# Moving the rounding of the quantised tiles in the loop from VectorE to ScalarE

## Chip, cores and metric

One core of one Trainium2 chip runs the kernel. The metric is the device time of the whole program in microseconds (us), lower is better; the time of a kernel is the median of its runs.

## What is computed

Input `x` has 4 batches of 1024 rows of width 512. Two layers follow each other. The first is a gated feed-forward layer with a quantised second half; the second is a small adapter whose weights depend on the batch.

```python
h = x * ((cond @ norm_w.T + 1)[:, None, :] * rsqrt(mean(x * x) + EPS))
val, gate = split(h @ up_w.T, 2)                    # up_w: 4096 x 512
h = val * gelu(gate)                                # 2048 wide
scale = 127 / clip(max(abs(h), axis=-1), 1e-5)      # one scale per row
hq = clip(round(h * scale), -128, 127) / scale      # act_quant
x1 = hq @ weight_quant(down_w).T + x                # 2048 -> 512
Wd_b = Wd + 0.1 * (cond @ Wdd.T + bdd)              # per batch, as for Wu_b
out = x1 + relu(x1 @ Wd_b.T + bd) @ Wu_b.T + bu
```

The step that matters here is `round(h * scale)`. The kernel rounds by adding and then subtracting 1.5 * 2^23 (`ROUND`) in float32. The result is an integer that bf16 holds exactly, so the second product runs in bf16.

## The kernel before, in words

The 4096 rows of `x` are worked on in eight chunks (c = 0 to 7) of 512 rows. Within a chunk, 16 steps (j = 0 to 15) each make one 128 x 512 tile of `h`. Chunk 0 also prepares the weights. Chunks 1 to 6 are three iterations of a loop with two chunks in its body, and chunk 7 stands behind the loop. The quantisation and the down projection of a chunk are done while the next chunk's steps run: tiles of chunk c-1 are quantised in steps 0 to 7 of chunk c, two tiles a step, and multiplied by the down weights in steps 9 to 12.

Each engine has its own queue, and its order is written out by hand (`run` in each engine's block). In a step of chunks 1 to 6 it is as follows.

- **TensorE** (`run`, L953): twelve float16 products for the gate tile (`up_products`, L889 to L895), then twelve for the value tile. It needs the gelu of two steps before (L965) and the `h` tile of two steps before (L987), because the PSUM tiles have two buffers each. In step 0, `turn_absrun` and `spread_scales` stand behind the two halves. In steps 7, 9, 11, 13 and 15 `delta_products` (L897 to L907) follows the value tile; it waits until VectorE has transposed four units of adapter weights (`nat_turned`). In steps 9 to 12 come 16 bf16 products of the down projection (L950), which wait for all of `q_done` (L943).
- **ScalarE** (`run`, L498): gelu of the gate tile into `g` (L507), in step 0 then the copy of the scales (`copy_scales`, L488), then `abs` of the finished `h` tile into the same `g` buffer (L516), which waits for `h_done`. In steps 2 to 5 it also squares a tile of the next `x` (L454), in steps 7 and 8 it scales two of them (L459).
- **VectorE** (`run`, L699): first the transposes of adapter weights (`turn_nat`, L675): in chunks 1 to 6 two instructions in each of steps 4 to 7 and four in each of steps 8 to 15; in chunk 7 only steps 8 to 11 have any. Then `quantise` (L655) in steps 0 to 7: two products by the scale (L660) and two roundings that add and subtract in one instruction and write bf16 (L663). Then the product of value, descale and gelu into `h[j]` (L739), which waits for TensorE, for the gelu and, because it overwrites the tile of the chunk before, for `q_done` of tile j (L738). Then the running maximum of `abs` (L751), which waits for ScalarE's `abs_done`.
- **SyncE** starts the DMAs; it reloads a buffer of adapter weights when it has been transposed (L337).

The tiles of the last chunk are quantised behind the loop by `quantise_last` on VectorE (L830) and `round_tiles` on ScalarE (L570): VectorE rounds the even tiles, ScalarE the odd ones, each in two ACTIVATE instructions.

Of the kernel before, what the change touches and what calls it, by code (L numbers as in the profile page):

```python
# [9 lines left out]
ALU = mybir.AluOpType  # L10
ACT = mybir.ActivationFunctionType
# [4 lines left out]
ROUND = 1.5 * 2.0 ** 23  # L16
# [6 lines left out]
def conditioned_block(nc, x, cond, norm_w, up_w, down_w, Wd, bd, Wu, bu, Wdd, bdd, Wdu, bdu, out):  # L23
# [6 lines left out]
    NCH = N // CH  # L30
    TT = CH // P
    KD = D // P
    FT = FF // P
# [14 lines left out]
    with ExitStack() as ctx:  # L48
        def sb(name, shape, dt):
            return ctx.enter_context(nc.sbuf_tensor(name, shape, dt))  # L50

        def sem(name):
            return ctx.enter_context(nc.semaphore(name))
# [10 lines left out]
        h = sb("h", [P, FT, CH], F32)  # L64
        qreg = sb("qreg", [P, FT * CH // 2], F32)
        q = qreg[:, :].bitcast(BF16).rearrange("p (f t) -> p f t", f=FT)
# [54 lines left out]
        def piece(p):  # L121
            o = 3072 + (p % 2) * 512
            return qreg[:, o:o + 512]
# [4 lines left out]
        def down_rows(dt):  # L128
            o = (4, 8, 12, 8)[dt]
            return h[:, o:o + 4, :].rearrange("p a b -> p (a b)")  # L130
# [44 lines left out]
        h_scaled, q_done = sem("h_scaled"), sem("q_done")  # L175
# [10 lines left out]
        round_added, q_done_act = sem("round_added"), sem("q_done_act")  # L186
# [11 lines left out]
        def squares_in(c, j):  # L198
            return [t for t, a in enumerate((0, 0, 1, 1) if is_first(c) else (2, 3, 4, 5)) if a == j]

        def scalings_in(c, j):
            return [t for t, a in enumerate((2, 2, 3, 3) if is_first(c) else (7, 7, 8, 8)) if a == j]

        def turn_in(c, j):
            k = j - (4 if is_first(c) else 10)
            return [k] if 0 <= k < KD else []
# [4 lines left out]
        def is_first(c):  # L211
            return isinstance(c, int) and c == 0
# [17 lines left out]
        def batch_at(c, last, j):  # L230
            return [u // 4 for u in units_at(c, last, j) if u % 4 == 3]

        def batch_of(i, par, beta):
            k = beta if par else LOOP_UNITS // 4 + beta
            return 10 * i + k, k % 2, 5 * i + k // 2
# [211 lines left out]
        def _(act):  # L447
            def square_x(n, par, t):
                if is_first(n):
                    act.wait_ge(x0_in[t], 16)  # L450
                elif t == 0:
                    act.wait_ge(x_in, 16 * n)
                    act.wait_ge(x_rstd, n)
                act.activation(xl[:, par, t, :].bitcast(BF16), xn[:, t, :], ACT.Square, accum_out=ss[:, t:t + 1]).then_inc(x_squared, 1)  # L454

            def scale_x(n, t):
                if t == 0:
                    act.wait_ge(x_rstd, n + 1)
                act.activation(xn[:, t, :], xn[:, t, :], ACT.Copy, scale=rstd[:, t:t + 1]).then_inc(x_scaled, 1)  # L459

            def x_hi(c, par, k):
                if k == 0:
                    act.wait_ge(sc_copied, c + 2)
                act.wait_ge(ta_full, ta_x(c, k) + 1)
                act.activation(xh[:, par, k, :], x_bank(c, k)[:, :], ACT.Copy, scale=sc_now[:, k:k + 1]).then_inc(x_hi_done, 1)  # L465

            def w_square(jj):
                act.wait_ge(upn_in[jj % 3], 32 * (jj // 3 + 1))
                for i in range(2):
                    m = 2 * jj + i  # L470
                    if m > 0:
                        act.wait_ge(w_squared, m)
                    act.activation(xr[:, 1, :], upn(jj, i), ACT.Square, accum_out=wss[:, m:m + 1]).then_inc(w_squared, 1)

            def w_hi_half(jj):
                for i in range(2):
                    m, ft = 2 * jj + i, jj + FT * i
                    act.wait_ge(w_turned, m + 1)
                    act.activation(w_hi[:, :, ft * P:(ft + 1) * P],
                                   w_bank(jj)[i][:, :].rearrange("p (k f) -> p k f", k=KD), ACT.Copy).then_inc(w_hi_done, 1)  # L480

            def copy_pieces(i):
                dt, f0 = i // 2, 8 * (i % 2)
                act.wait_ge(ta_full, TA_PIECE + i + 1)
                act.activation(wqT[:, f0:f0 + 8, dt * P:(dt + 1) * P],
                               TA[:, :].bitcast(BF16).rearrange("p (f d) -> p f d", f=8), ACT.Copy).then_inc(ta_freed, 1)

            def copy_scales(c):  # L488
                act.wait_ge(s_turned, c + 1)
                act.activation(s_bc[:, :], TB[:, :], ACT.Copy).then_inc(s_bc_done, 1)  # L490
# [7 lines left out]
            def run(c, par, b, i):  # L498
                first, last = is_first(c), b is None
                for j in range(FT):  # L500
                    n = FT * c + j
                    act.wait_ge(gate_full, n + 1)
                    if first:
                        act.wait_ge(desc_done, max(1, j - 1))
                    if not (first and j < 2):
                        act.wait_ge(max_done, n - 1)
                    act.activation(g[:, j % 2, :], GATE[j % 2][:, :], ACT.Gelu,  # L507
                                   scale=desc[:, 2 * j + 1:2 * j + 2]).then_inc(gelu_done, 1)
                    if first and j + 2 < FT:
                        w_hi_half(j + 2)  # L510
                    if first and j + 3 < FT:
                        w_square(j + 3)
                    if not first and j == 0:
                        copy_scales(c - 1)
                    act.wait_ge(h_done, n + 1)
                    act.activation(g[:, j % 2, :], h[:, j, :], ACT.Abs).then_inc(abs_done, 1)  # L516
                    if not last:
                        for t in squares_in(c, j):
                            square_x(c + 1, 1 - par, t)
                        for t in scalings_in(c, j):  # L520
                            scale_x(c + 1, t)
                        for k in turn_in(c, j):
                            x_hi(c, 1 - par, k)
                    if first and 7 <= j < 15:
                        for p in (2 * (j - 7), 2 * (j - 7) + 1):
                            act.wait_ge(piece_in[p % 2], 16 * (p // 2 + 1))
                            if p == 0:
                                act.wait_ge(mean_step, 3)
                            act.activation(piece(p), piece(p), ACT.Copy, scale=wtot[:, 2:3], bias=ROUND).then_inc(piece_biased, 1)
                    if first and j >= 8:  # L530
                        copy_pieces(j - 8)
                    if first and j < 6:
                        for m in {4: (4, 5), 5: (6, 7)}.get(j, (j,)):
                            act.wait_ge(rows_in[m // 2], 16)
                            half = down_rows(m // 2)[:, FF // 2 * (m % 2):FF // 2 * (m % 2 + 1)]
                            act.activation(half, half, ACT.Abs, accum_out=wabs[:, m:m + 1]).then_inc(rows_summed, 1)
                    for beta in batch_at(c, last, j):
                        if batch_of(i, par, beta)[1] == 1:
                            read_sums(i, par, beta)
# [30 lines left out]
            def round_tiles(m0, m1):  # L570
                for m in range(m0, m1):
                    k = 2 * m + 1
                    act.wait_ge(h_scaled, FT * (NCH - 1) + k + 1)
                    act.activation(h[:, k, :], h[:, k, :], ACT.Copy, bias=ROUND).then_inc(round_added, 1)
                    act.wait_ge(round_added, m + 1)
                    act.activation(q[:, k, :], h[:, k, :], ACT.Copy, bias=-ROUND).then_inc(q_done_act, 1)

            act.wait_ge(bd_in, 16)
            copy_x1(0, 0)
            copy_x1(1, 1, (0, 1))  # L580
            copy_scales(NCH - 1)
            copy_x1(1, 1, (2, 3))
            round_tiles(0, 1)
# [13 lines left out]
        def _(dve):  # L597
# [57 lines left out]
            def quantise(c, k0):  # L655
                if k0 == 0:
                    dve.wait_ge(s_bc_done, c + 1)

                for k in (k0, k0 + 1):
                    dve.tensor_tensor(h[:, k, :], h[:, k, :], s_bc[:, :], ALU.mult).then_inc(h_scaled, 1)  # L660
                for k in (k0, k0 + 1):
                    dve.wait_ge(h_scaled, FT * c + k + 1)
                    dve.tensor_scalar(q[:, k, :], h[:, k, :], ROUND, ROUND, ALU.add, ALU.subtract).then_inc(q_done, 1)  # L663

            def quant_pieces(i):
                for p in (2 * i, 2 * i + 1):
# [445 lines left out]
```

## Time and profile before

| what | value |
|---|---|
| median of 3 runs | 1034.6 us |
| lowest, highest | 1031.19, 1034.74 us |
| the profiled execution, its own time | 1033.38 us |
| its span in the trace | 1031.6 us |
| mean granted TensorE clock | 0.993 of full speed |
| busy: TensorE, VectorE, ScalarE | 966.2, 681.9, 329.8 us |

The span is the time between the first and the last instruction in the trace; the execution's own time has 1.8 us around it. Busy time of TensorE comes from modelled ends of pipelined instructions, so consecutive matmuls overlap in the records: what a matmul costs is the distance from its start to the next one's. The same holds in a smaller measure on VectorE and ScalarE, where an instruction may start before the end of the one ahead of it. In timelines, equal instructions that follow each other are merged (x2, x4) and the time given is from the first start to the last end.

### The profile page before, as it was taken

What the parts mean: (1) busy time and instruction counts of PE and PEld (TensorE: products, weight loads), DVE (VectorE), ACT (ScalarE), POOL (GpSimd) and SP (SyncE); (2) the same over time, 40 slices, a digit from 0 to 9 for tenths busy, and PEclk for the clock granted to TensorE, in tenths of its full rate; (3) what the DMA queues carried; (4) which work ended last, traced back from release to release, by engine and by line L of the source; (5) the groups of instructions that cost most, each with busy time, mean ns of one, the idle gap of its engine ahead of it and who ended that gap; (6) DMA issues with size and microseconds to landing.
All of it is one profiled execution on the core that took longest, in us unless ns stands there. A gap on an engine that the chain in (4) does not pass through costs nothing.

```text
span 1031.6 us, 14604 instructions
## 1 busy us (share of the span) xinstructions
PE 966.2 (94%) x5307; PEld 467.7 (45%) x5307; DVE 681.9 (66%) x1138; ACT 329.8 (32%) x599; POOL 51.3 (5%) x53
## 2 busy tenths in 40 slices
PE   1899999999999989999999899999999999987998
PEld 1555544444444444444444344444444444444454
DVE  1878758766785748766885658756876677428433
ACT  2797832312321222212322223222332222115222
POOL 1000000000000000000000000000000000004153
PEclk9999999999999999999999999999999999989999
DMA  7442341545145412454145412544154512232365
GB/s 275 142 151 88 121 144 62 183 144 163 42 153 152 153 66 85 161 162 145 42 165 164 150 45 92 173 155 133 51 173 155 166 69 82 72 112 82 142 227 182
DMA packets 73314, 134.70 MB, mean 131 GB/s; under 512 B 5268, under 2 KB 10904, under 8 KB 72728
## 3 DMA queue, kind: packets, MB, share of 16 engines
q1 hardware_dynamic: 73240, 133.72, 39.5%
q8 instruction: 46, 0.75, 0.3%
q14 instruction: 28, 0.23, 0.1%
HBM read 112.72 MB, written 20.97 MB: 130 GB/s over the span
## 4 chain that ended last, share of the span: by engine, by line
PE 74%; DVE 15%; issue 6%; ACT 2%; SPq 2%; DMA 1%; DVEq 0%; POOL 0%; ACTq 0%; POOLq 0%
PE bank L892 16%; PE bank L893 16%; PE bank L894 16%; PE bank L950 10%; DVE natT L681 8%; PE bank L905 6%; PE bank L1063 2%; PE bank L1048 2%; DVE h L739 2%; DVE h L660 2%; PE bank L877 1%; PE bank L867 1%; ACT g L516 1%; PE bank L1039 1%; DVE h L833 1%
## 5 line engine op out<-in xcount | busy, mean ns | idle before, releaser
L892 PE MATMUL bank<-x_split,w_hi 128*128 128x512 f16 x1024 | 390.4, 381 | 10.0 <-issue 7.4
L893 PE MATMUL bank<-x_split,w_hi 128*128 128x512 f16 x1024 | 390.0, 381 | 0.0
L894 PE MATMUL bank<-x_split,w_lo 128*128 128x512 f16 x1024 | 389.8, 381 | 0.0
L681 DVE STREAM_TRANSPOSE natT<-nat 128x512 f32<-128x512 f32 x256 | 249.6, 1087 | 1.2 <-PE bank L905 0.8
L516 ACT ACTIVATE g<-h 128x512 f32<-128x512 f32 x128 | 80.6, 630 | 362.3 <-DVE h L739 362.3
L739 DVE SCALAR_TENSOR_TENSOR h<-bank,desc,g 128x512 f32<-128x512 f32 x128 | 94.8, 740 | 106.0 <-issue 66.3
L892 PEld LDWEIGHTS bank<-x_split,w_hi 128*128 128x128 f16 x1024 | 100.7, 98 | 129.9 <-issue 17.3
L894 PEld LDWEIGHTS bank<-x_split,w_lo 128*128 128x128 f16 x1024 | 100.7, 98 | 122.2 <-issue 2.5
L507 ACT ACTIVATE g<-bank,desc 128x512 f32<-128x512 f32 x128 | 87.3, 682 | 208.6 <-PE bank L894 208.6
L893 PEld LDWEIGHTS bank<-x_split,w_hi 128*128 128x128 f16 x1024 | 100.7, 98 | 115.1 <-issue 1.9
L751 DVE TENSOR_TENSOR absrun<-absrun,g 128x512 f32<-128x512 f32 x120 | 83.0, 691 | 75.1 <-ACT g L516 75.1
L950 PE MATMUL bank<-wqT,qreg 128*128 128x512 bf16 x512 | 115.3, 379 | 0.0
L660 DVE TENSOR_TENSOR h<-h,s_bc 128x512 f32<-128x512 f32 x112 | 71.6, 680 | 15.5 <-ACT s_bc L490 15.5
L905 PE MATMUL bank<-natT,cond_diag 128*32 128x256 f32 x1024 | 61.9, 382 | 18.1 <-DVE natT L681 18.1
L950 PEld LDWEIGHTS bank<-wqT,qreg 128*128 128x128 bf16 x512 | 49.5, 98 | 57.5 <-issue 3.3
L905 PEld LDWEIGHTS bank<-natT,cond_diag 128*32 128x32 f32 x1024 | 30.3, 109 | 49.2 <-issue 18.7
L828 DVE TENSOR_TENSOR w_hi<-bank,w_hi 128x512 f32<-128x512 f32 x32 | 21.7, 687 | 34.0 <-PE bank L1063 34.0
L421 POOL TENSOR_TENSOR rstd<-ss,mhalf 128x4 f32<-128x4 f32 x8 | 8.1, 1014 | 725.3 <-DVE ss L630 713.6
L663 DVE TENSOR_SCALAR qreg<-h 128x512 bf16<-128x512 f32 x112 | 42.0, 417 | 0.0
L1063 PE MATMUL bank<-natT,w_lo 128*128 128x512 f32 x64 | 30.7, 609 | 4.8 <-DVE w_hi L828 4.1
L696 DVE SCALAR_TENSOR_TENSOR xr<-bank,fy,xr 128x512 f32<-128x512 f32 x32 | 22.3, 697 | 17.8 <-PE bank L950 10.9
L641 DVE SCALAR_TENSOR_TENSOR x_split<-bank,sc_now,x_split 128x512 f16<-128x512 f32 x32 | 23.6, 746 | 12.9 <-ACT x_split L465 12.9
(118 smaller groups left out, 543.7 us busy)
## 6 DMA issues: line engine op xcount, KB each, us to landing
nat<-in_L_cond_Wdd SPq DMA_DIRECT2D x64, 512.0 KB, 3.6
nat<-in_L_cond_Wdu SPq DMA_DIRECT2D x64, 512.0 KB, 3.5
qreg<-in_L_cond_up_w SPq DMA_DIRECT2D x32, 256.0 KB, 4.3
xr<-in_x SPq DMA_DIRECT2D x32, 256.0 KB, 4.6
x_scratch<-xr SPq DMA_DIRECT2D x32, 256.0 KB, 4.8
xn<-in_x SPq DMA_DIRECT2D x7, 1024.0 KB, 6.4
out_y<-w_hi SPq DMA_DIRECT2D x7, 1024.0 KB, 4.3
h<-in_L_cond_down_w SPq DMA_DIRECT2D x4, 1024.0 KB, 7.6
```

The costliest lines, as they stand in the source:

```text
L507: act.activation(g[:, j % 2, :], GATE[j % 2][:, :], ACT.Gelu, scale=desc[:, 2 * j + 1:2 * j + 2]).then_inc(gelu_done, 1)
L516: act.activation(g[:, j % 2, :], h[:, j, :], ACT.Abs).then_inc(abs_done, 1)
L660: dve.tensor_tensor(h[:, k, :], h[:, k, :], s_bc[:, :], ALU.mult).then_inc(h_scaled, 1)
L681: last = dve.transpose(natT[:, t, kk, :, :].rearrange("p a (r e) -> p e a r", e=4), nat[:, t, kk, :])
L739: dve.scalar_tensor_tensor(h[:, j, :], VAL[j % 2][:, :], desc[:, 2 * j:2 * j + 1], g[:, j % 2, :], ALU.mult, ALU.mult).then_inc(h_done, 1)
L751: dve.tensor_tensor(absrun[:, :], absrun[:, :], g[:, j % 2, :], ALU.max).then_inc(max_done, 1)
L892: pe.matmul(bank[:, :], w_hi[:, k, cols], xh[:, par, k, :], start=(k == 0), stop=False)
L893: pe.matmul(bank[:, :], w_hi[:, k, cols], xl[:, par, k, :], start=False, stop=False)
L894: mm = pe.matmul(bank[:, :], w_lo[:, k, cols], xh[:, par, k, :], start=False, stop=(k == KD - 1))
L905: mm = pe.matmul(HY[32 * t:32 * t + 32, cols], cond_diag[:, a, :], natT[:, t, :, a, :], start=(a == 0), stop=(a == HB - 1))
L950: mm = pe.matmul(bank[:, :], q[:, f, t * P:(t + 1) * P], wqT[:, f, :], start=(f == 0), stop=(f == FT - 1))
L1063: pe.matmul(up_bank[t][:, :], down_T[:, par, t * P:(t + 1) * P], wu_all[:, b, :], start=True, stop=True).then_inc(up_full, 1)
```

## The change

VectorE's two rounding instructions of each pair of tiles are gone. ScalarE gets, in steps 0 to 7 of chunks 1 to 7, four instructions per step between its gelu (in step 0: behind the copy of the scales) and its `abs`: add `ROUND` in place in float32 for both tiles, then subtract it into the bf16 tile for both. Each addition waits for VectorE's product of that tile, each subtraction for its own addition. `q_done` is now counted up by ScalarE. The tiles of the last chunk are quantised as before; only the count that `round_tiles` waits for starts at another base, since the loop now counts the same semaphore.

```diff
--- before.py
+++ after.py
@@ -485,6 +485,14 @@
                 act.activation(wqT[:, f0:f0 + 8, dt * P:(dt + 1) * P],
                                TA[:, :].bitcast(BF16).rearrange("p (f d) -> p f d", f=8), ACT.Copy).then_inc(ta_freed, 1)
 
+            def round_pair(c, k0):
+                for k in (k0, k0 + 1):
+                    act.wait_ge(h_scaled, FT * c + k + 1)
+                    act.activation(h[:, k, :], h[:, k, :], ACT.Copy, bias=ROUND).then_inc(round_added, 1)
+                for k in (k0, k0 + 1):
+                    act.wait_ge(round_added, FT * c + k + 1)
+                    act.activation(q[:, k, :], h[:, k, :], ACT.Copy, bias=-ROUND).then_inc(q_done, 1)
+
             def copy_scales(c):
                 act.wait_ge(s_turned, c + 1)
                 act.activation(s_bc[:, :], TB[:, :], ACT.Copy).then_inc(s_bc_done, 1)
@@ -512,6 +520,8 @@
                         w_square(j + 3)
                     if not first and j == 0:
                         copy_scales(c - 1)
+                    if not first and j < 8:
+                        round_pair(c - 1, 2 * j)
                     act.wait_ge(h_done, n + 1)
                     act.activation(g[:, j % 2, :], h[:, j, :], ACT.Abs).then_inc(abs_done, 1)
                     if not last:
@@ -572,7 +582,7 @@
                     k = 2 * m + 1
                     act.wait_ge(h_scaled, FT * (NCH - 1) + k + 1)
                     act.activation(h[:, k, :], h[:, k, :], ACT.Copy, bias=ROUND).then_inc(round_added, 1)
-                    act.wait_ge(round_added, m + 1)
+                    act.wait_ge(round_added, FT * (NCH - 1) + m + 1)
                     act.activation(q[:, k, :], h[:, k, :], ACT.Copy, bias=-ROUND).then_inc(q_done_act, 1)
 
             act.wait_ge(bd_in, 16)
@@ -658,9 +668,6 @@
 
                 for k in (k0, k0 + 1):
                     dve.tensor_tensor(h[:, k, :], h[:, k, :], s_bc[:, :], ALU.mult).then_inc(h_scaled, 1)
-                for k in (k0, k0 + 1):
-                    dve.wait_ge(h_scaled, FT * c + k + 1)
-                    dve.tensor_scalar(q[:, k, :], h[:, k, :], ROUND, ROUND, ALU.add, ALU.subtract).then_inc(q_done, 1)
 
             def quant_pieces(i):
                 for p in (2 * i, 2 * i + 1):
```

## Rows read from the trace of the kernel before

**Rows 1.** Page, part 1: engine, busy us (share of span) xinstructions.

```profile
PE 966.2 (94%) x5307; PEld 467.7 (45%) x5307; DVE 681.9 (66%) x1138; ACT 329.8 (32%) x599; POOL 51.3 (5%) x53
```

**Rows 2.** Groups by line: busy us, mean ns of one | idle before, releaser.

```profile
L905 PE MATMUL bank<-natT,cond_diag 128*32 128x256 f32 x1024 | 61.9, 382 | 18.1 <-DVE natT L681 18.1
...
L663 DVE TENSOR_SCALAR qreg<-h 128x512 bf16<-128x512 f32 x112 | 42.0, 417 | 0.0
```

**Rows 3.** TensorE's waits in chunk 3 (365:478 us): total us, times, longest.

```profile
PE bank L905 <- DVE natT L681: 2.8, 3, 1.0
```

**Rows 4.** TensorE's timeline, chunk 3: start us, us, instruction [idle before <-releaser].

```profile
409.60 1.93 PE L905 MATMUL bank<-natT,cond_diag 128*32 128x256 f32 x32 [0.95 <-DVE natT L681]
411.47 0.39 PE L892 MATMUL bank<-x_split,w_hi 128*128 128x512 f16 x1
...
422.93 1.93 PE L905 MATMUL bank<-natT,cond_diag 128*32 128x256 f32 x32 [0.93 <-DVE natT L681]
```

**Rows 5.** VectorE's timeline, chunk 3, steps 4 to 10.

```profile
389.47 0.69 DVE L751 TENSOR_TENSOR absrun<-absrun,g 128x512 f32<-128x512 f32 x1 [0.69 <-ACT g L516]
390.08 2.03 DVE L681 STREAM_TRANSPOSE natT<-nat 128x512 f32<-128x512 f32 x2
391.94 1.27 DVE L660 TENSOR_TENSOR h<-h,s_bc 128x512 f32<-128x512 f32 x2
...
393.79 0.74 DVE L739 SCALAR_TENSOR_TENSOR h<-bank,desc,g 128x512 f32<-128x512 f32 x1
395.23 0.69 DVE L751 TENSOR_TENSOR absrun<-absrun,g 128x512 f32<-128x512 f32 x1 [0.70 <-ACT g L516]
...
412.59 0.69 DVE L751 TENSOR_TENSOR absrun<-absrun,g 128x512 f32<-128x512 f32 x1 [0.70 <-ACT g L516]
...
433.69 0.75 DVE L739 SCALAR_TENSOR_TENSOR h<-bank,desc,g 128x512 f32<-128x512 f32 x1 [4.28 <-PE bank L894]
```

**Rows 6.** ScalarE's timeline, chunk 3, steps 3 and 4.

```profile
388.81 0.63 ACT L516 ACTIVATE g<-h 128x512 f32<-128x512 f32 x1 [2.74 <-DVE h L739]
389.34 0.61 ACT L454 ACTIVATE x_split<-xn 128x512 bf16<-128x512 f32 x1
...
394.57 0.63 ACT L516 ACTIVATE g<-h 128x512 f32<-128x512 f32 x1 [3.32 <-DVE h L739]
```

**Rows 7.** ScalarE's timeline after the loop: its own roundings.

```profile
943.09 0.63 ACT L574 ACTIVATE h<-h 128x512 f32<-128x512 f32 x1 [1.45 <-DVE h L833]
943.75 0.63 ACT L576 ACTIVATE qreg<-h 128x512 bf16<-128x512 f32 x1
```

**Rows 8.** ScalarE's timeline after the last step: four PSUM copies in a row.

```profile
934.24 2.05 ACT L562 ACTIVATE w_hi<-bank 128x512 f32<-128x512 f32 x4
```

**Rows 9.** VectorE's timeline, chunk 3, steps 0 to 3.

```profile
373.06 1.29 DVE L660 TENSOR_TENSOR h<-h,s_bc 128x512 f32<-128x512 f32 x2 [2.21 <-ACT s_bc L490]
...
376.38 0.43 DVE L748 COPY absrun<-g 128x512 f32<-128x512 f32 x1 [0.69 <-ACT g L516]
376.72 1.29 DVE L660 TENSOR_TENSOR h<-h,s_bc 128x512 f32<-128x512 f32 x2
...
382.84 0.75 DVE L739 SCALAR_TENSOR_TENSOR h<-bank,desc,g 128x512 f32<-128x512 f32 x1 [0.24 <-issue]
...
388.02 0.75 DVE L739 SCALAR_TENSOR_TENSOR h<-bank,desc,g 128x512 f32<-128x512 f32 x1 [1.17 <-issue]
```

**Rows 10.** VectorE's timeline, last chunk, step 4.

```profile
847.06 0.75 DVE L739 SCALAR_TENSOR_TENSOR h<-bank,desc,g 128x512 f32<-128x512 f32 x1 [1.17 <-issue]
```

**Rows 11.** TensorE's timeline at the start of chunk 3, after its longest idle time.

```profile
364.49 0.38 PE L892 MATMUL bank<-x_split,w_hi 128*128 128x512 f16 x1 [4.09 <-issue]
...
368.76 0.60 PE L930 MATMUL bank<-identf,absrun 128*128 128x128 f32 x4
```

**Rows 12.** Windows: busy us (x) of each engine, granted clock, DMA share, GB/s.

```profile
365.00:370.00 5.00, 5.00 (x19) 2.18 (x18) 0.60 (x1) 0.69 (x1) 0.00 (x0) 0.66 0.40 152
...
405.00:410.00 5.00, 4.05 (x25) 1.76 (x27) 4.30 (x8) 1.21 (x2) 0.00 (x0) 1.00 0.33 102
```

## The prediction

> **What bounds the kernel now.** The page's part 1 comes first [rows 1]: TensorE is busy 94% of the span, VectorE 66%, ScalarE 32%. So only TensorE's idle time can be won, and only new idle time on it can be lost; work moved from VectorE to ScalarE is worth what it changes there. The groups by line say who makes TensorE wait in the loop [rows 2]: the adapter products L905 lose 18.1 us to VectorE's transposes. One chunk's waits [rows 3] show the pattern: three stops, 2.8 us together. The other loop chunks repeat it.
>
> TensorE's timeline gives the places [rows 4]: 0.95 us idle before the L905 group of step 7, 0.93 us before that of step 9. It also gives its pace: from 411.47 to the idle time's start (422.00) run the 48 products of steps 8 and 9; the last starts 0.38 us before its modelled end, so 47 distances fill 10.15 us, 0.216 us each. A step of 24 takes 5.18 us.
>
> VectorE's timeline says why it is late [rows 5]. The running maximum L751 starts at 389.47 in step 3, at 395.23 in step 4 and at 412.59 in step 7: 5.76 to 5.80 us a step against TensorE's 5.18. These steps are a ring of two engines with no wait for TensorE in it: maximum, 0.61 us later two transposes, 1.86 later the two products by the scale, 1.85 later the h pass L739, then ScalarE's abs and the next maximum. ScalarE's rows close it [rows 6]: abs starts 0.04 us after the h pass ends, is 0.63 long, and the maximum follows 0.03 later. In step 10 VectorE waits 4.28 us for TensorE (the last of [rows 5]), so the lag of a chunk is paid by then and not carried on.
>
> **The change, part by part.** It removes 112 roundings of 0.417 us, 42.0 us of VectorE's time [rows 2], and adds 224 ACTIVATEs on ScalarE. Their form stands behind the loop [rows 7]: 0.63 us each, so 141 us more, and ScalarE goes from 329.8 to about 471 us busy, 46% of the span. Neither total is the price; the ring is.
>
> *The price that decides* is the distance between two independent ScalarE instructions. Three rows are near. Two with no wait for each other stand 0.53 apart (388.81 and 389.34 in [rows 6]); an addition and the subtraction that waits for it stand 0.66 apart [rows 7]; four copies in a row take 2.05 us [rows 8], which is 0.47 apart if the last runs 0.63. In a new pair each subtraction waits for an addition two places before it, long finished when its turn comes; the new instructions have rows 6's engine, tile and length. I take 0.53 and keep 0.47 and 0.66 as ends.
>
> *Steps 4 to 7.* Before, abs started 2.63 us after the first product by the scale (391.94 to 394.57). Now the second product ends at 1.27 and ScalarE's second addition starts 0.04 later (the first ran beside the second product). Two subtractions and the abs follow at 0.53 each: 1.27 + 0.04 + 3 x 0.53 = 2.90. VectorE's h pass runs meanwhile and is earlier than before, which helps nobody, because abs stands behind the roundings in ScalarE's queue, and VectorE's maximum and next transposes stand behind abs. Each step gets 0.27 us longer: 6.03 instead of 5.76. Step 7's transposes come after three such steps, so TensorE's stop there grows by 0.81 to about 1.76 us. Step 7 adds the fourth, and the L905 group of step 9 comes 1.08 us later. There it ends: step 10's 4.28 us of waiting absorb no shift of TensorE itself, but keep VectorE from adding more.
>
> *Steps 0 to 3* are covered, narrowly [rows 9]. In step 0 the h pass now waits for a subtraction: 373.06 + 1.29 + 0.04 + 0.53 + 0.63 + 0.03 = 375.58, and the maximum of step 0 starts at 377.03 instead of 376.38. Steps 1 to 3 each run maximum to products (0.34 in step 1, then 0.61), products to abs (1.33 + 1.59), abs to maximum (0.66), and abs of step 3 could start at 388.67. It could not start before 388.81 anyway: its h pass waits for TensorE until 388.02. The cover is 0.14 us; gone if the distance is over 0.544, since ten distances lie on this path. TensorE needs nothing of step 0 before step 2 (h pass at 382.84, waiting for it).
>
> *Chunk 7* has no transposes in steps 4 to 7; before, its h passes waited 1.17 us for TensorE [rows 10], more than the 0.27. Cost nothing. The final rounding behind the loop issues the same instructions; its new count costs nothing.
>
> *DMAs.* No DMA is added. SyncE reloads adapter weights when they are transposed, up to 1.08 us later, but they are used four units on, at least two steps of over 5 us; nothing.
>
> The sum: six chunks (1 to 6) x 4 x 0.27 = 6.5 us. Against the profiled execution's 1033.38 that is 1039.9; that run lies 1.2 below the median of 1034.6, so the forecast is 1041.1. With 0.47 a step grows by 0.09 and the sum is 2.2 us (1036.8). With 0.66 it grows by 0.66, the start adds 1.3 - 0.14 = 1.16 per chunk, and the sum is 6 x (2.64 + 1.16) = 22.8 us (1057.4).
>
> By rows, a rounding costs VectorE 0.42 us and ScalarE 0.63 twice. The Trainium skill (ScalarE: Activation LUTs, Rules for kernel authors) sends additions to VectorE rather than ScalarE, which speaks against this change; if each step were charged the full difference of engine time, 4 x 0.63 - 2 x 0.417 = 1.69 us, 24 steps would cost 40 us. The rows make it 6.5, because most of the roundings lies beside the h pass.
>
> **The rivals.**
>
> *Small lag.* The distance is under 0.51, the lag per step under 0.22 us and the sum under 5.2. For it: copies at 0.47 to 0.51 [rows 8]. Against: those read PSUM. About 1038.
>
> *Not slower.* ScalarE's three distances hide behind the h pass. It decides at 0.44: there 1.31 + 3 x 0.44 = 2.63, the old length. If the roundings were wholly hidden, VectorE's missing 0.66 would bring steps 4 to 7 to 5.10 us, under TensorE's 5.18, and the 0.95 us stop of step 7 would go, six times: 5.7 us, 1028.9. No SBUF row runs that close.
>
> *Dear distance.* Waits on its own additions keep ScalarE from overlapping, 0.66 apart: up to 1057. For it: rows 7; against: there the awaited instruction is the one just before.
>
> *The clock.* After the longest idle time in the loop, 4.09 us, twelve products took 4.27 us instead of 12 x 0.216 = 2.59 [rows 11], and the granted clock of that stretch was 0.66 [rows 12], part of it at 1.2 GHz. After 0.95 us idle it stayed at 1.00. If 1.76 us were enough to let it fall, step 8's value tile would be full at 411.47 + 0.81 + 1.68 + 5.18 + 0.16 = 419.30, when VectorE could have used it at 412.59 + 1.08 + 0.61 + 2 x 1.86 = 418.00: 1.30 more per chunk, 7.8 us in all, 1048.9. The Trainium skill (TensorE: Matmul & The Clock Gate, HAM oscillation) describes kernels that pay the warm-up anew after every such gap; no row here shows it for so short a one.
>
> *The change does nothing*, because the lag of steps 4 to 7 is not the one TensorE waits for: against it, the two stops stand exactly at VectorE's transposes.
>
> **How the numbers follow.** A measurement of this kernel can tell about 0.5%, 5.2 us, from no change. Forecast (5.2 to 11 us more): 0.58. Small lag 0.19. Not slower 0.05, of which 0.04 below the bound. Dear distance 0.07. Clock 0.07. Nothing 0.04. So slower is 0.72, faster 0.04, same 0.24. The range goes from 1036.5 (the 0.47 end) to 1049.5 (the clock case); it leaves out the hidden case, some of the small ones, and most of the dear ones.
>
> **What would show it.** In the changed profile: VectorE about 640 us busy, ScalarE about 471; L905 waiting for transposes about 18.1 + 6.5 = 24.6 us, the stop of step 7 about 1.76 us, that of step 9 about 1.2; maxima in steps 4 to 7 of chunks 1 to 6 at 6.03 us, in chunk 7 unchanged; h passes of step 3 still waiting for TensorE; subtraction to subtraction and subtraction to abs 0.53 apart. Wrong if abs waits for the h pass in steps 4 to 7 as before, if the clock falls in step 8, or if step 3 no longer waits for TensorE.

## Result and the profile after

The changed kernel takes 1039.93 us (median of 5 runs, 1039.01 to 1044.26) against 1034.22 us of the kernel before in the same runs: a ratio of 1.0068, 95% interval 1.0043 to 1.0094. A second set of runs of the same kernel, taken with the experiments, gave 1039.64 us and 1.0069 (1.0051 to 1.0086). The forecast was 1041.1 us, a ratio of 1.0063.

Part 1 of the page after, which answers to [rows 1]:

```profile
PE 965.2 (93%) x5277; PEld 467.2 (45%) x5307; DVE 645.6 (62%) x1026; ACT 450.5 (43%) x823; POOL 51.3 (5%) x53
```

TensorE's work is unchanged: the 30 matmuls fewer (x5277) are records missing from the trace, which has 482 of the 512 products of the down projection, while all 5307 weight loads are there. VectorE lost 36 us of busy time, ScalarE gained 121. The groups by line (busy us, mean ns of one | idle time before, releaser) show the two new groups, and the adapter products that answer to the first of [rows 2]:

```profile
L491 ACT ACTIVATE h<-h 128x512 f32<-128x512 f32 x112 | 68.4, 629 | 65.4 <-DVE h L670 65.4
L494 ACT ACTIVATE qreg<-h 128x512 bf16<-128x512 f32 x112 | 63.4, 613 | 0.0
L912 PE MATMUL bank<-natT,cond_diag 128*32 128x256 f32 x1024 | 61.9, 382 | 24.2 <-DVE natT L688 24.2
```

The products waited 18.1 us for the transposes before and wait 24.2 us now, 6.1 more. The median grew by 5.7. The span of this execution is 1042.4 us, 10.8 over the one of before; it was the longest of its five (1044.26 us). Of the 10.8 us, 4.05 lie ahead of chunk 1, which began at 143.10 us in it and at 139.05 before, and 6.8 between there and the end of chunk 7. Nothing of the change lies ahead of chunk 1. A further profile of the same kernel, with a span of 1036.3 us, begins chunk 1 at 139.55; the timelines below are from that one. Among all profiles taken, edited or not, this start lies between 138.5 and 143.1 us with no relation to the edit, so chunks are compared from their own start here.

VectorE's timeline of chunk 3, from the h pass of step 3 to the maximum of step 7, in that second profile (start us, us, instruction [idle before <-releaser]); it answers to [rows 5]:

```profile
391.21 0.75 DVE L746 SCALAR_TENSOR_TENSOR h<-bank,desc,g 128x512 f32<-128x512 f32 x1 [1.17 <-PE bank L901]
392.66 0.69 DVE L758 TENSOR_TENSOR absrun<-absrun,g 128x512 f32<-128x512 f32 x1 [0.70 <-ACT g L526]
393.27 2.03 DVE L688 STREAM_TRANSPOSE natT<-nat 128x512 f32<-128x512 f32 x2
395.13 1.28 DVE L670 TENSOR_TENSOR h<-h,s_bc 128x512 f32<-128x512 f32 x2
396.39 0.75 DVE L746 SCALAR_TENSOR_TENSOR h<-bank,desc,g 128x512 f32<-128x512 f32 x1
398.67 0.69 DVE L758 TENSOR_TENSOR absrun<-absrun,g 128x512 f32<-128x512 f32 x1 [1.53 <-ACT g L526]
...
404.68 0.69 DVE L758 TENSOR_TENSOR absrun<-absrun,g 128x512 f32<-128x512 f32 x1 [1.60 <-ACT g L526]
...
416.72 0.69 DVE L758 TENSOR_TENSOR absrun<-absrun,g 128x512 f32<-128x512 f32 x1 [1.60 <-ACT g L526]
```

Step 3's h pass still waits 1.17 us for TensorE. The maxima then stand 6.01, 6.01, 6.09 and 5.95 us apart, 24.06 us for four steps, where it was 23.12 (389.47 to 412.59 in [rows 5]): 0.235 more per step. The idle time before each maximum rose from 0.70 to 1.53 or 1.60 us. That is the gap in which VectorE, early with its h pass, waits for an abs that stands behind four roundings. ScalarE's timeline of steps 3 and 4, which answers to [rows 6]:

```profile
392.00 0.63 ACT L526 ACTIVATE g<-h 128x512 f32<-128x512 f32 x1 [0.25 <-DVE h L746]
...
395.85 1.23 ACT L491 ACTIVATE h<-h 128x512 f32<-128x512 f32 x2 [1.52 <-DVE h L670]
396.99 1.13 ACT L494 ACTIVATE qreg<-h 128x512 bf16<-128x512 f32 x2
398.02 0.61 ACT L526 ACTIVATE g<-h 128x512 f32<-128x512 f32 x1
```

The abs of step 4 has no idle time before it: it starts when ScalarE is through with the subtractions, 1.63 us after the h pass (396.39), and no longer 0.78 after it. From the first product by the scale (395.13) to abs it is 2.89 us, where the prediction worked out 2.90. The two subtractions and the abs follow each other at 0.52 us (396.99, one more, 398.02).

TensorE's timeline of the same chunk shows where it lands, as in [rows 4]:

```profile
413.49 1.93 PE L912 MATMUL bank<-natT,cond_diag 128*32 128x256 f32 x32 [1.76 <-DVE natT L688]
...
427.03 1.93 PE L912 MATMUL bank<-natT,cond_diag 128*32 128x256 f32 x32 [1.14 <-DVE natT L688]
```

The stop of step 7 is 1.76 us (0.95 before), that of step 9 is 1.14 (0.93 before); the forecast was 1.76 and 1.2. In the six chunks of the first profile the stop of step 7 lies between 1.56 and 1.78 us. Summed over these six chunks, the stop of step 7 has grown by 4.5 us, that of step 9 by 1.3 and a third one, that of step 15, by 0.3: together the 6.1. Chunk 7 has no transposes in steps 4 to 7, and its h passes wait even longer for TensorE than in [rows 10], here in step 4:

```profile
852.73 0.75 DVE L746 SCALAR_TENSOR_TENSOR h<-bank,desc,g 128x512 f32<-128x512 f32 x1 [1.84 <-issue]
```

### The profile page after: what moved, and what is told of

Same layout as the page of the kernel before. It is cut to its first block, busy times and chain, and to the rows that moved or that the text cites. A ratio compares the mean times of both kernels' runs of the same rounds, so it can differ in the third digit from the quotient of the medians.

```text
span 1042.4 us, 14734 instructions
## 1 busy us (share of the span) xinstructions
PE 965.2 (93%) x5277; PEld 467.2 (45%) x5307; DVE 645.6 (62%) x1026; ACT 450.5 (43%) x823; POOL 51.3 (5%) x53
## 4 chain that ended last, share of the span: by engine, by line
PE 69%; DVE 15%; issue 7%; ACT 6%; SPq 2%; DMA 1%; DVEq 0%; POOL 0%; ACTq 0%; POOLq 0%
PE bank L899 15%; PE bank L900 15%; PE bank L901 14%; PE bank L957 10%; DVE natT L688 8%; PE bank L912 5%; DVE h L670 2%; PE bank L1070 2%; PE bank L1055 2%; ACT g L526 2%; ACT h L491 1%; PE bank L884 1%; ACT qreg L494 1%; PE bank L874 1%; DVE h L746 1%
## 5 line engine op out<-in xcount | busy, mean ns | idle before, releaser
L688 DVE STREAM_TRANSPOSE natT<-nat 128x512 f32<-128x512 f32 x256 | 249.7, 1087 | 1.2 <-PE bank L912 0.8
L957 PE MATMUL bank<-wqT,qreg 128*128 128x512 bf16 x482 | 111.2, 379 | 2.4 <-issue 1.3
L491 ACT ACTIVATE h<-h 128x512 f32<-128x512 f32 x112 | 68.4, 629 | 65.4 <-DVE h L670 65.4
L912 PE MATMUL bank<-natT,cond_diag 128*32 128x256 f32 x1024 | 61.9, 382 | 24.2 <-DVE natT L688 24.2
L494 ACT ACTIVATE qreg<-h 128x512 bf16<-128x512 f32 x112 | 63.4, 613 | 0.0
```

The lines of the kernel that those rows point to most:

```text
L688: last = dve.transpose(natT[:, t, kk, :, :].rearrange("p a (r e) -> p e a r", e=4), nat[:, t, kk, :])
L912: mm = pe.matmul(HY[32 * t:32 * t + 32, cols], cond_diag[:, a, :], natT[:, t, :, a, :], start=(a == 0), stop=(a == HB - 1))
L957: mm = pe.matmul(bank[:, :], q[:, f, t * P:(t + 1) * P], wqT[:, f, :], start=(f == 0), stop=(f == FT - 1))
```

## The experiments

Each was timed side by side with the kernel before on the same chip, in three sets, in which the kernel before took 1034.17, 1035.46 and 1034.76 us; the ratios are formed within a set and need not be those of the medians. As a second measure, free of the noise ahead of chunk 1, I give the distance between the first VectorE instruction of `finish_max` in chunk 1 and in chunk 2: one undisturbed loop chunk. The kernel before has 112.26 us there.

| kernel | ratio to before (95%) | median us | chunk 1 to 2, us |
|---|---|---|---|
| changed, again | 1.0069 (1.0051 to 1.0086) | 1039.64 | 113.31 |
| ScalarE in steps 0 to 3 only | 1.0005 (0.9992 to 1.0019) | 1034.06 | 112.40 |
| ScalarE in steps 4 to 7 only | 1.0063 (1.0047 to 1.0080) | 1040.08 | 113.30 |
| one tile of two on ScalarE | 0.9962 (0.9949 to 0.9976) | 1031.52 | 112.04 |
| ScalarE, one step later | 0.9953 (0.9934 to 0.9971) | 1028.63 | 111.43 |
| the same, again | 0.9940 (0.9918 to 0.9962) | 1027.99 | 111.47 |
| VectorE, behind its h pass | 0.9918 (0.9902 to 0.9935) | 1026.84 | 111.25 |
| the same, again | 0.9941 (0.9918 to 0.9965) | 1027.06 | 111.25 |
| one more, ahead of abs | 1.0223 (1.0199 to 1.0247) | 1060.06 | 116.40 |
| one more, right behind abs | 1.0093 (1.0073 to 1.0113) | 1046.19 | 115.36 |
| one more, behind the square too | 1.0052 (1.0034 to 1.0071) | 1040.16 | 113.36 |

**The changed kernel again.**

> The changed kernel once more, unedited, for a second profile. Theory (the lag of steps 4 to 7, about 0.24 us a step in chunks 1 to 6): about 6 us over the kernel before, 1040; chunk lengths as in the first profile, and the start of chunk 1 back near 139 us, since nothing of the change lies in chunk 0. Rival (the change also costs about 4 us in chunk 0): the start of chunk 1 stays near 143 us and the time near 1044.

It was 1039.64 us, and chunk 1 began at 139.55 us. The 4 us ahead of chunk 1 in the first profile belong to that execution, not to the change.

**Which steps pay.** Two kernels leave one half of the roundings on VectorE (the counts that are waited for are changed to fit):

```diff
-                    if not first and j < 8:
+                    if not first and 0 <= j < 4:        # the other kernel: 4 <= j < 8
                         round_pair(c - 1, 2 * j)
...
+                if k0 >= 8:                             # the other kernel: k0 < 8
+                    for k in (k0, k0 + 1):
+                        dve.wait_ge(h_scaled, FT * c + k + 1)
+                        dve.tensor_scalar(q[:, k, :], h[:, k, :], ROUND, ROUND, ALU.add, ALU.subtract).then_inc(q_done, 1)
```

> ScalarE rounds only in steps 0 to 3, VectorE as before in steps 4 to 7. Theory: the delay in steps 0 to 3 is covered by TensorE's pace (step 3 still waits for the value tile), so the time is the kernel before's, 1034, within 1 us. Rival (every rounding moved costs alike): half of the change, 1037.

> ScalarE rounds only in steps 4 to 7, VectorE as before in steps 0 to 3. Theory: the whole cost is here, 6 us more than before, 1040. Rival (every rounding moved costs alike): half, 1037.

Both came out as the theory had it: nothing that the timing can tell for steps 0 to 3 (1.0005), the full cost for steps 4 to 7 (1.0063). The trace does show a little for steps 0 to 3: 0.14 us in chunk 1 to 2 (112.40 against 112.26), under 1 us for six chunks. In chunks 1, 3 and 5 the h pass of step 3 starts 18.73 us after the chunk's start there, and 18.62 before, although TensorE's products stand at the same places; why is open. TensorE's waits for VectorE's transposes over the whole span (total us, times, longest us), first with ScalarE in steps 0 to 3:

```profile
PE bank L916 <- DVE natT L692: 18.6, 19, 1.4
```

and with ScalarE in steps 4 to 7:

```profile
PE bank L916 <- DVE natT L692: 24.1, 19, 1.7
```

The same number of roundings was moved in both. A price for each rounding moved is out.

**The order on ScalarE.** Each pair but the first is rounded one step later, still between gelu and abs:

```diff
-                    if not first and j < 8:
-                        round_pair(c - 1, 2 * j)
+                    if not first and (j == 0 or 2 <= j < 9):
+                        round_pair(c - 1, 2 * max(0, j - 1))
```

> The same four ScalarE instructions per pair, but each pair one step later (pair 0 in step 0, pair k in step k+1), between gelu and abs as in the change. They then run while VectorE transposes and multiplies and no longer hold back abs. Theory (the order matters: abs standing behind roundings whose input comes late): steps 4 to 7 shrink to about 5.1 us on VectorE's side, under TensorE's 5.18, TensorE's stop in step 7 goes, about 0.95 us per chunk is won against the kernel before: 1034.2 - 5.7 = 1028.5, that is 11 to 12 us under the changed kernel. Rival (ScalarE's added 141 us as such, or both engines at work in SBUF, is what costs): about the changed kernel's time, 1040, since the work is the same.

ScalarE does the same work and the kernel is faster than both others: 1028.63 us, ratio 0.9953. ScalarE's timeline of step 4:

```profile
390.15 0.69 ACT L515 ACTIVATE g<-bank,desc 128x512 f32<-128x512 f32 x1 [0.41 <-PE bank L901]
390.74 1.14 ACT L491 ACTIVATE h<-h 128x512 f32<-128x512 f32 x2
391.77 1.14 ACT L494 ACTIVATE qreg<-h 128x512 bf16<-128x512 f32 x2
393.70 0.63 ACT L526 ACTIVATE g<-h 128x512 f32<-128x512 f32 x1 [0.79 <-DVE h L746]
```

The additions start behind gelu with no wait, since their input is a step old. ScalarE is through with them at 392.91, and abs waits another 0.79 us for the h pass, no longer for the roundings. TensorE's adapter products in the same chunk:

```profile
408.17 1.93 PE L912 MATMUL bank<-natT,cond_diag 128*32 128x256 f32 x32
...
421.63 1.93 PE L912 MATMUL bank<-natT,cond_diag 128*32 128x256 f32 x32 [1.06 <-DVE natT L688]
```

The first group (step 7) has no idle time before it; the stop of step 9 stays, at 1.06 us. The prediction's faster rival had worked out just this (the 0.95 goes, step 9 keeps its own), for a case in which the roundings hide; here they do.

**Less of it.** ScalarE takes only the odd tile of each pair (against the kernel before; the waits for `q_done` are split between it and `q_odd`):

```diff
                 for k in (k0, k0 + 1):
                     dve.tensor_tensor(h[:, k, :], h[:, k, :], s_bc[:, :], ALU.mult).then_inc(h_scaled, 1)
-                for k in (k0, k0 + 1):
-                    dve.wait_ge(h_scaled, FT * c + k + 1)
-                    dve.tensor_scalar(q[:, k, :], h[:, k, :], ROUND, ROUND, ALU.add, ALU.subtract).then_inc(q_done, 1)
+                dve.wait_ge(h_scaled, FT * c + k0 + 1)
+                dve.tensor_scalar(q[:, k0, :], h[:, k0, :], ROUND, ROUND, ALU.add, ALU.subtract).then_inc(q_done, 1)
...
+            def round_odd(c, k0):
+                k = k0 + 1
+                act.wait_ge(h_scaled, FT * c + k + 1)
+                act.activation(h[:, k, :], h[:, k, :], ACT.Copy, bias=ROUND).then_inc(round_added, 1)
+                act.wait_ge(round_added, FT // 2 * c + k0 // 2 + 1)
+                act.activation(q[:, k, :], h[:, k, :], ACT.Copy, bias=-ROUND).then_inc(q_odd, 1)
```

> Of each pair, VectorE rounds the even tile as before and ScalarE the odd one (two instructions in place of four). Theory (only what stands between the second product and abs counts, on the longer of the two ways): ScalarE's way is 1.27 + 0.04 + 0.66 (the subtraction waits for the addition ahead of it) + 0.53 = 2.50 us from the first product to abs, VectorE's 1.19 + 0.33 + 0.74 + 0.04 = 2.30; the longer is 0.13 under the 2.63 of the kernel before, so steps 4 to 7 run at 5.63 us and the time is 4 x 6 x 0.13 = 3.1 us under the kernel before: 1031. Rival (a price for each rounding moved): half of the change, 1037.

The time is 1031.52 us, ratio 0.9962: less than before, as the longer of the two ways had it, and on the other side of 1 from what half of the change would cost. Its adapter products in step 7:

```profile
409.83 1.93 PE L913 MATMUL bank<-natT,cond_diag 128*32 128x256 f32 x32 [0.54 <-DVE natT L689]
```

The stop went from 0.95 to 0.54 us: three steps of 0.14 against the 0.13 worked out. The chunk itself, though, shrank by 0.22 us only (112.26 to 112.04), not by 4 x 0.13 = 0.52. From step 8 on TensorE's value tile is the later of the two: VectorE reaches the maximum of step 7 0.57 us earlier than in the kernel before, counted from the chunk's start (42.63 against 43.20), and the one of step 8 only 0.33 earlier (48.64 against 48.97). So the trace gives about 1.3 us for six chunks and the timing 2.5 to 5.3 us; which part of that difference is noise of the runs stays open.

**No move at all.** The kernel before, with VectorE's two roundings behind its h pass from step 1 on:

```diff
                 for k in (k0, k0 + 1):
                     dve.tensor_tensor(h[:, k, :], h[:, k, :], s_bc[:, :], ALU.mult).then_inc(h_scaled, 1)
+                if k0 == 0:
+                    round_both(c, k0)
+
+            def round_both(c, k0):
                 for k in (k0, k0 + 1):
                     dve.wait_ge(h_scaled, FT * c + k + 1)
...
                     dve.scalar_tensor_tensor(h[:, j, :], VAL[j % 2][:, :], desc[:, 2 * j:2 * j + 1], g[:, j % 2, :],
                                              ALU.mult, ALU.mult).then_inc(h_done, 1)
+                    if not first and 1 <= j < 8:
+                        round_both(c - 1, 2 * j)
```

> The kernel before with one edit: from step 1 on VectorE's two roundings stand behind its h pass instead of ahead of it; nothing is moved to ScalarE. They then fall into the 0.7 us in which VectorE waits for abs. Theory (position, not engine): steps 4 to 7 need 5.10 us, the stop of step 7 goes, 1028.5, the same as with the roundings one step later on ScalarE. Rival (VectorE's busy time is what has to shrink): the kernel before's time, 1034, since VectorE is as busy as before.

The ratio was 0.9918, and 0.9941 (0.9918 to 0.9965) in a second set of runs. VectorE is as busy as before (685 us) and the kernel is 6 to 8.5 us faster by these ratios. The trace accounts for the smaller figure: a chunk is 1.01 us shorter (111.25 against 112.26), 6.1 us for six. Its timeline in a step with transposes, from the products by the scale to the next transposes:

```profile
388.57 1.25 DVE L660 TENSOR_TENSOR h<-h,s_bc 128x512 f32<-128x512 f32 x2
389.81 0.75 DVE L743 SCALAR_TENSOR_TENSOR h<-bank,desc,g 128x512 f32<-128x512 f32 x1
390.48 0.75 DVE L667 TENSOR_SCALAR qreg<-h 128x512 bf16<-128x512 f32 x2
391.25 0.69 DVE L757 TENSOR_TENSOR absrun<-absrun,g 128x512 f32<-128x512 f32 x1
391.87 2.02 DVE L685 STREAM_TRANSPOSE natT<-nat 128x512 f32<-128x512 f32 x2
```

The roundings fill 390.48 to 391.23, and the maximum follows at once; in the kernel before 0.70 us of idle time stood there [rows 5]. From maximum to maximum such steps now take 5.18 us: TensorE's pace.

Both versions once more, side by side:

> The version with VectorE's roundings behind its h pass once more, side by side with the next. Theory: 5.7 us under the kernel before (ratio 0.9945), and the same as the next one within 1 us, since in both TensorE sets the pace of steps 4 to 7. Rival (ScalarE's 141 us more slow VectorE's own instructions a little, as its 4 us more of busy time in the first trace of the next one hint): this one is 1 to 3 us faster than the next.

> The version with ScalarE's roundings one step later, side by side with the one before. Theory: the same time within 1 us. Rival: 1 to 3 us slower.

0.9941 and 0.9940, each known to about 0.0023 (2.4 us): no difference that can be measured, though the rival's 1 us is not excluded by it. The profiles still show 649 us of busy time on VectorE with ScalarE's roundings one step later, against 646 in the changed kernel, which has the same VectorE instructions (a product by the scale takes 701 ns there instead of 682, a transpose 1098 instead of 1087), and loop chunks of 111.47 us against 111.25 (chunks 1, 3 and 5; chunk 6 is 111.27 and 111.25), which makes under 1 us in all. It is small and mostly hidden.

**More of it, in two places.** One subtraction is done twice in each of steps 4 to 7 (the result is the same), either ahead of abs or right behind it. Its first time counts a semaphore of its own, `spare_done`, and from step 8 on VectorE's h pass waits for all of `q_done`:

```diff
+            def again(c, j):
+                k = 2 * j                               # the kernel with it behind abs: 2 * j + 1
+                act.wait_ge(spare_done, 4 * c + j - 3)
+                act.activation(q[:, k, :], h[:, k, :], ACT.Copy, bias=-ROUND).then_inc(q_done, 1)
...
                         round_pair(c - 1, 2 * j)
+                    if not first and 4 <= j < 8:        # the other kernel: behind the abs
+                        again(c - 1, j)
```

> The changed kernel with one subtraction done twice in each of steps 4 to 7, ahead of abs. Theory: each of these steps gets 0.52 us longer, 4 x 6 x 0.52 = 12.5 us more than the changed kernel, 1052; the stop of step 7 grows from 1.8 to 3.4 us, and if the clock falls after that (it did after 4.09 and 3.28 us), 1.3 to 1.7 us more in each of six chunks, up to 1062. Rival (ScalarE's load): the same as with the instruction behind abs.

> The same instruction more, but behind abs. Theory: nothing, 1040, since ScalarE then stands 2 us idle until VectorE's next product. Rival (ScalarE's load): the same as with the instruction ahead of abs.

Ahead of abs: ratio 1.0223, that is 0.0154 over the changed kernel's 1.0069, some 16 us (19 by the medians), between the 12.5 and the 22 that were worked out. TensorE's timeline of chunk 3 has both parts of it:

```profile
422.08 2.43 PE L920 MATMUL bank<-natT,cond_diag 128*32 128x256 f32 x32 [3.31 <-DVE natT L696]
...
424.84 0.63 PE L908 MATMUL bank<-x_split,w_hi 128*128 128x512 f16 x1
425.27 0.63 PE L909 MATMUL bank<-x_split,w_lo 128*128 128x512 f16 x1
...
427.11 0.38 PE L908 MATMUL bank<-x_split,w_hi 128*128 128x512 f16 x1
427.32 0.38 PE L909 MATMUL bank<-x_split,w_lo 128*128 128x512 f16 x1
```

3.31 us idle (3.11 to 3.37 in the six chunks), and then products that start 0.43 us apart, until at 427.11 they are back at 0.21. The window over this stretch (its length, busy us and count of PE, PEld, DVE, ACT, POOL, then the granted clock, DMA share, GB/s) has a granted clock of 0.72:

```profile
424.00:429.00 5.00, 5.00 (x24) 1.86 (x17) 3.17 (x4) 3.64 (x7) 0.00 (x0) 0.72 0.36 116
```

So the products at 0.43 us ran at 1.2 GHz, those at 0.21 at 2.4 GHz. The clock fell like this in five of the six chunks.

Behind abs: 1.0093, not the 1.0069 expected. The two intervals just overlap; the chunks do not leave it open (115.36 us against 113.31). This miss has two parts. The first is on VectorE, in step 5:

```profile
408.30 0.69 DVE L766 TENSOR_TENSOR absrun<-absrun,g 128x512 f32<-128x512 f32 x1 [1.60 <-ACT g L532]
409.43 0.17 DVE L648 TENSOR_SCALAR ss<-ss 128x4 f32<-128x4 f32 x1 [0.44 <-ACT x_split L455]
409.52 2.03 DVE L696 STREAM_TRANSPOSE natT<-nat 128x512 f32<-128x512 f32 x2
```

The small instruction that sums up the squares of `x` (L648, `mean_square`) waits 0.44 us for ScalarE, whose square of `x` stands behind the added instruction. VectorE's transposes, and with them TensorE's stop, come later by that. I had taken ScalarE's idle time ahead of the next product as free, and had overlooked that something else in that stretch is waited for. The second part is the clock. The stop of step 7 is 2.27 us in chunk 1 and 2.29 in chunk 3:

```profile
180.70 3.27 PE L920 MATMUL bank<-natT,cond_diag 128*32 128x256 f32 x32 [2.27 <-DVE natT L696]
```

```profile
417.64 1.93 PE L920 MATMUL bank<-natT,cond_diag 128*32 128x256 f32 x32 [2.29 <-DVE natT L696]
```

The first group takes 3.27 us, the second 1.93. The windows behind them in chunk 1

```profile
178.00:183.00 5.00, 2.73 (x30) 1.34 (x32) 4.33 (x6) 2.92 (x6) 0.00 (x0) 0.81 0.19 68
```

and in chunk 3

```profile
419.00:424.00 5.00, 5.00 (x33) 2.16 (x26) 3.40 (x5) 4.16 (x8) 0.00 (x0) 1.00 0.43 152
```

say why: 0.81 of full speed in one, 1.00 in the other. The clock fell in chunks 1, 2 and 6 and held in 3, 4 and 5, with stops between 2.07 and 2.36 us in all six. Chunk 1, with the fall, took 115.36 us, and chunk 3, without it, 113.81: the fall costs about 1.5 us, the later transposes 0.4 to 0.5. For six chunks and three falls that is about 7 us over the changed kernel, where the ratios give 2.5 and the medians, each against its kernel before, 5.3. The profiled execution has the lowest granted clock of its four (0.985 against 0.988 and 0.989), so the others may have had less of the fall. Both parts can be taken away by a place further back:

> The changed kernel with one subtraction done twice in steps 4 to 7, now behind abs and behind the square of x as well. Theory (ahead of the square it made VectorE's mean_square wait 0.44 us in step 5, and lengthened the stop of step 7 so far that the clock fell in three of six chunks): here neither, so the changed kernel's time, ratio 1.0069 to the kernel before, 1041, and no fall of the clock. Rival (ScalarE's load itself costs): as with the instruction straight behind abs, 1.009.

1.0052 (1.0034 to 1.0071), no fall of the clock behind these stops, and TensorE's waits over the span are those of the changed kernel:

```profile
PE bank L920 <- DVE natT L696: 24.6, 19, 1.8
```

So ScalarE's load as such costs nothing that can be measured: its busy time rose by another 14 us, and the time did not.

## Why the prediction was right

**The bound.** It said that only TensorE's idle time before the adapter products of steps 7 and 9 can grow. The idle time before these products grew by 6.1 us and the median by 5.7. Right in the main: 5.8 of the 6.1 stand before steps 7 and 9. The remaining 0.3 stand before step 15, the third of the three stops of [rows 3], which the prediction did not follow.

**The price of a step.** It took 0.53 us between ScalarE instructions and got 2.90 us from product to abs; the trace has 0.52 and 2.89. The lag per step was put at 0.27 and is 0.235: 0.01 lies in the distances, 0.02 in the abs itself, which is recorded with 0.61 us where it follows another instruction and with 0.63 where it starts after idle time, and the rest is within the rounding of the rows. Four steps make 0.94 instead of 1.08, six chunks 5.6 instead of 6.5 us. A whole loop chunk nevertheless grew by 1.05 (113.31 against 112.26), because in chunks 1, 3 and 5 the h pass of step 3 and the stop of step 15 add about 0.1 us each. Neither was in the prediction, so that the growth of a chunk comes so near to 1.08 is in part luck. The upper end of 0.66 (waits keep ScalarE from overlapping) fell: a subtraction whose addition stands two places ahead does not slow down.

**Steps 0 to 3.** The cover of 0.14 us is there in chunks 2, 4 and 6: abs of step 3 starts 3.04 us after the first product, where the roundings would let it start after 2.90. In chunks 1, 3 and 5 it is 3.24 us, so there was more room. The kernel with ScalarE in these steps only, at 1.0005, shows that the cover holds, but for the 0.1 us named above.

**Chunk 7.** As predicted, nothing: its h passes wait for TensorE in steps 4 to 7.

**The ring.** The view that position decides, not the engine, is borne out from four sides: more roundings ahead of abs cost more, the same roundings one step later win 5 to 6 us against the kernel before, half of them wins a little, and VectorE's own roundings moved behind its h pass win as much or more, without any work moved to another engine.

**The rivals.** The clock stayed at 2.4 GHz behind the stops of 1.56 to 1.78 us of the changed kernel. That rival was wrong here, but not by much: behind stops of 2.1 to 2.4 us it already fell in three chunks of six. (Its row for the short stop, 405 to 410 in [rows 12], ends 0.4 us behind that stop and says little; the window from 410 to 415 has 1.00 too.) Its price was near: with one more instruction ahead of abs, chunk 1, with the fall, took 116.40 us and chunk 5, in which the clock held, 115.30, so the fall costs 1.1 us, and 1.5 with the instruction behind abs, against the 1.3 worked out. The rival that was not slower had the right mechanism for another kernel: its 5.7 us and 1028.9 us are what the version with the later rounding measured (1028.63).

**Busy times** were forecast as 640 and 471 us and came out as 646 and 451. I added up full durations, but neighbours overlap by 0.1 us and busy time counts an overlap once. It touched no term of the sum.

**The Trainium skill's rule** that an addition belongs on VectorE (ScalarE: Activation LUTs, Rules for kernel authors) gave the right sign. Read as engine time by the prediction, 40 us, it was seven times too much. The runs agree with it only where ScalarE's roundings stand ahead of abs in the ring: one step later the two engines cannot be told apart (0.9940 and 0.9941).

## What to carry to other kernels

When work moves between two engines that wait for each other in turn, write down the ring (what must end before the other can start, and what stands ahead of it in its queue) and add up the longer way; busy time does not give the price. Ask first whether the work needs to be in the ring at all: here a version as fast as any leaves it on the same engine and puts it into the idle 0.7 us in which that engine waits for the other. Moving a step of work by one iteration, so that its input is old when its turn comes, does the same on the other engine.

## What the runs showed of the hardware that was not expected

- TensorE's clock fell from 2.4 to 1.2 GHz in three of six chunks with idle times of 2.07 to 2.36 us before the adapter products, in five of six with 3.11 to 3.37 us, and in none with 1.55 to 1.82 us (18 chunks: the changed kernel twice, and the one with the instruction behind the square too). The one of those six in which it held had 3.30 us. Equal idle times (2.27 and 2.29 us) had different outcomes within one execution.
- In the kernel that rounds one step later on ScalarE, VectorE's instructions are slightly slower than in the changed kernel: 701 ns instead of 682 for a 128x512 float32 product by the scale. ScalarE's roundings run beside them there; that this is the cause was not shown.
- The start of chunk 1 wanders by up to 4.6 us between executions (138.5 to 143.1 us); a single profile with a longer span must not be read as the effect of an edit before that is ruled out.
